# Four groups a turn in TensorE's loop, and the next group's transposes ahead of the last output projection

## The chip, the core and the metric

The kernel runs on one core of a Trainium2 chip. The metric is the device time of one execution in microseconds. A core has five engines that run their own instruction streams and meet only at semaphores: TensorE (PE: matmuls and transposes, which write to the PSUM banks), VectorE (DVE), ScalarE (ACT), GpSimd (POOL) and SyncE (SP), which here issues all the DMAs.

## What is computed

Eight sequences of 1024 tokens with 256 features each go through two "macaron" layers, all in float32:

```
x = x + 0.5 * ffn0(layernorm(x))          # gated silu, hidden size 768
x = x + delta_net(layernorm(x))           # 16 heads, conv, gated recurrence over time, out projection
x = x + 0.5 * ffn0(layernorm(x))
x = x + 0.5 * ffn1(layernorm(x))          # token shift, sigmoid(r) * (relu(k)^2 @ W_v)
x = x + block_attention(layernorm(x))     # 16 heads, rope, causal blocks of 64
x = x + 0.5 * ffn1(layernorm(x))
```

## The kernel before

The 8192 tokens are worked on in 16 groups of 512 tokens, two to a sequence. A group passes through these stages on TensorE, in this order of code:

1. `ffn()`: the normalised rows XN of the group are transposed into PSUM banks 0 and 1 (`transposes()`, eight 128x128 transposes). ScalarE copies bank 0 and VectorE bank 1 into XT (`xt_copy()` on each), and `xt_both()` waits for both copies. Then come the gate and up matmuls of the first feed-forward layer, six times two pairs of 128x512, and the down projection.
2. A second `transposes()` with `xt_both()` for the delta net's input, then the decay inputs and 32 projections with their convolution (`projections`), and the preparation of the chunks' matrices.
3. `recurrence`: eight chunks of 64 tokens, with a chain between TensorE, VectorE and ScalarE. At its end the last chunk's output is normalised by VectorE, transposed by TensorE into bank 2 (`output_t`), copied to VO by ScalarE (`copied()` on TensorE waits for that), and multiplied with WO (`projected(NT - 1)`: 16 matmuls, which the trace shows as 32 records). VectorE adds the result to x, and `added()` on TensorE waits for this addition.

All that comes after the delta net for a group (the second feed-forward layer, the shifted one, the attention and the last one) is called the tail. It is a generator on each engine, cut into 49 pieces, and the pieces of the group before are put into the gaps of the current group's recurrence (`FILL`). All 49 are used up before the last output is transposed, so `for _ in rest` at the end of `recurrence` has nothing left. After the loop the tail of the last group runs by itself.

The next group's x is loaded into R during the recurrence. VectorE takes its statistics before the last output's normalisation and writes XN right behind it (`input_stats`, `input_normal`), ahead of the addition of the last projection.

Loops: TensorE, ScalarE and GpSimd each have a loop of 16 turns with one group a turn. VectorE's has 8 turns of two groups, with two memsets at the head of a turn. SP's has 7 turns of two groups. A loop ends in a branch back to its first instruction. The boundary between two groups is called a seam below. On TensorE it is this order of work:

```
output_t(CHUNKS - 1, 1)
copied()
projected(NT - 1)
added()
pe.wait_ge(s_ready, 2)      # banks 0 and 1 are free again
(branch back)
transposes()                # waits for XN
xt_both()                   # waits for both copies to XT
first gate matmul
```

The loop on TensorE is left after the 16th group; the code behind it starts with two other transposes ("x0f", "x1f") that wait for VectorE's work on the last group.

Of the kernel before, what the change touches and what calls it, by code (L numbers as in the profile page):

```python
# [74 lines left out]
def bass_macaron(nc, x_in, w_gate, w_up, w_down, wq, wk, wv, wab, a_log, dt_bias, wo, conv_w,  # L75
                 w_qk, w_va, w_out, w_r, w_k, w_v, mu, consts, out):
    ctx = ExitStack()
    with ctx:
# [386 lines left out]
        def _(dve):  # L465
# [33 lines left out]
            def input_normal():  # L499
                normal(0, R, XN, xn_ready)  # L500
                normal(1, R, XN, xn_ready)

            def first_ffn(x):
                xt_copy()
                for m in range(HT):
                    s = m % 2
                    dve.wait_ge(th_ready, 1)
                    dve.sem_inc(th_ready, -1)
                    v.scalar_tensor_tensor(FTMP[:, s * G:s * G + G], FTH[:, s * G:s * G + G], 1.0, bank(2 + s),
                                           ALU.add, ALU.mult)  # L510
                    dve.drain()
                    dve.wait_ge(up_ps, 1)
                    dve.sem_inc(up_ps, -1)
                    v.tensor_tensor(out=HH[:, m * G:m * G + G], in0=FTMP[:, s * G:s * G + G], in1=bank(4 + s),
                                    op=ALU.mult).then_inc(h_ready, 1)
                for k in range(2):
                    cols = slice(2 * D * k, 2 * D * k + 2 * D)
                    dve.wait_ge(down_ps, 1)
                    dve.sem_inc(down_ps, -1)
                    if k == 0:  # L520
                        dve.wait_ge(xs_free, 1)
                        dve.sem_inc(xs_free, -1)
                    i = v.scalar_tensor_tensor(x[:, cols], bank(6 + k), 0.25 * W_SCALE ** 3, R[:, cols], ALU.mult, ALU.add)
                    if k == 1:
                        i.then_inc(x_used, 1)
                    dve.drain()
                    stats(k, x)
                for k in range(2):
                    normal(k, x, XN, xn_ready)
# [415 lines left out]
            def recurrence(p):  # L945
                rest = tail(1 - p)

                def fill(n):
                    for _ in range(n):
                        next(rest)  # L950

                fill(FILL_FIRST)
                keys(0)
                for c in range(CHUNKS):
                    right_side(c, 0)
                    right_side(c, 1)
                    fill(FILL[c][0])
                    fill(FILL[c][1])
                    if c >= 5:
                        projected(c - 5, XS[p])  # L960
                    s_update(c, 0)
                    s_update(c, 1)
                    if c + 1 < CHUNKS:
                        keys(c + 1)
                    if c >= 1:
                        mean_square(c - 1)
                    if c == CHUNKS - 1:
                        dve.drain().then_inc(r_free, 1)
                    fill(FILL[c][2])
                    if c >= 1:  # L970
                        normalise(c - 1, 0)
                        normalise(c - 1, 1)
                fill(FILL[CHUNKS][0])
                mean_square(CHUNKS - 1)
                input_stats()
                normalise(CHUNKS - 1, 0)
                normalise(CHUNKS - 1, 1)
                input_normal()
                projected(NT - 1, XS[p])
                dve.drain()  # L980
                for _ in rest:
                    pass
# [11 lines left out]
            dve.drain()  # L994
            input_stats()
            input_normal()
            with dve.Fori(0, B) as b:
                v.memset(S[:, 0:PAIRS * DV], 0.0)
                v.memset(HIST[:, :], 0.0)
                dve.drain()  # L1000
                for p in range(2):
                    first_ffn(XS[p])
                    xt_copy()
                    decay_and_beta()
                    projections(XS[1 - p])
                    recurrence(p)
# [205 lines left out]
        def _(act):  # L1212
# [5 lines left out]
                a.activation(XT[:, 1:G + 1], bank(0), ACT.Copy).then_inc(xt_act, 1)  # L1218

            def ffn():  # L1220
                xt_copy()
                for m in range(HT):
                    s = m % 2
                    act.wait_ge(gate_ps, 1)
                    act.sem_inc(gate_ps, -1)
                    a.activation(FTH[:, s * G:s * G + G], bank(2 + s), ACT.Tanh, scale=0.5 * W_SCALE).then_inc(th_ready, 1)
# [168 lines left out]
            def recurrence():  # L1395
                rest = tail()

                def fill(n):
                    for _ in range(n):
                        next(rest)  # L1400

                def output(c, x):
                    act.wait_ge(ot_ps, 1)
                    act.sem_inc(ot_ps, -1)
                    a.activation(VO[:, :].rearrange("p (n t) -> p n t", n=H)[:, 8 * x:8 * x + 8, c * C:c * C + C],
                                 v3(bank(2), 8), ACT.Copy).then_inc(ot_free, 1)

                def square_out(c, x):
                    act.wait_ge(o_ps, 1)
                    act.sem_inc(o_ps, -1)  # L1410
                    a.activation(SQO[c][:, 512 * x:512 * x + 512], bank(3 + x), ACT.Square).then_inc(sqo_ready, 1)

                fill(FILL_FIRST)
                for y in range(2):
                    inverse_q(y, bank(2 + y))
                for y in range(2):
                    inverse_t(0, y, bank(2 + y))
                for c in range(CHUNKS):
                    if c == 4:
                        inverse_t(1, 1, bank(2))  # L1420
                        act.drain().then_inc(a_done, 1)
                    fill(FILL[c][0])
                    if c >= 2:
                        output(c - 2, 0)
                    if c == 3:
                        inverse_q(0, bank(2))
                    for x in range(2):
                        act.wait_ge(u_ps, 1)
                        act.sem_inc(u_ps, -1)
                        a.activation(US[c % 2][:, 512 * x:512 * x + 512], bank(x), ACT.Copy).then_inc(u_ready, 1)  # L1430
                    if c >= 1:
                        square_out(c - 1, 0)
                    if c >= 2:
                        output(c - 2, 1)
                    if c >= 1:
                        square_out(c - 1, 1)
                    fill(FILL[c][1])
                    if c == 3:
                        inverse_q(1, bank(2))
                    fill(FILL[c][2])  # L1440
                    if c == 3:
                        inverse_t(1, 0, bank(2))
                output(CHUNKS - 2, 0)
                square_out(CHUNKS - 1, 0)
                output(CHUNKS - 2, 1)
                square_out(CHUNKS - 1, 1)
                fill(FILL[CHUNKS][0])
                fill(FILL[CHUNKS][1])
                output(CHUNKS - 1, 0)
                fill(FILL[CHUNKS][2])  # L1450
                output(CHUNKS - 1, 1)
                for _ in rest:
                    pass

            def projections():
                for i in range(CONV_TILES + 5):
# [34 lines left out]

            act.wait_ge(loaded, 16 * N_LOADS)
            a.activation(NEGA[:, :], NEGA[:, :], ACT.Exp).then_inc(nega_ready, 1)
            with act.Fori(0, B * GROUPS) as n:
                ffn()
                xt_copy()
# [14 lines left out]
        def _(pe):  # L1511
# [22 lines left out]
                pe.sem_inc(xt_dve, -1)  # L1534

            def ffn():
                transposes()
                xt_both()
                for m in range(HT):
                    s = m % 2  # L1540
# [375 lines left out]
            def recurrence(rest):  # L1916
# [157 lines left out]
                fill(FILL[CHUNKS][2])  # L2074
                copied()
                output_t(CHUNKS - 1, 1)
                copied()
                projected(NT - 1)
                for _ in rest:
                    pass  # L2080
                added()
                pe.wait_ge(s_ready, 2)
                pe.sem_inc(s_ready, -2)

            pe.wait_ge(loaded, 16 * N_LOADS)
            pe.wait_ge(w_ready, 1)
            pe.sem_inc(w_ready, -1)
            with pe.Fori(0, B * GROUPS) as n:
                ffn()
                transposes()  # L2090
                xt_both()
                pe.wait_ge(qkv_back, 32)
                pe.sem_inc(qkv_back, -32)
                decay_inputs()
                late = tail()
                projections(late)
                pe.wait_ge(b56_free, 2)
                pe.sem_inc(b56_free, -2)
                recurrence(late)
            transposed("x0f", LXN)  # L2100
            transposed("x1f", LXN)
            for _ in tail():
# [72 lines left out]
```

## Time and profile before

| | |
|---|---|
| time, median of 3 runs | 8546.34 us (8544.98 to 8560.92) |
| the profiled execution | 8542.67 us, its span in the profile 8540.9 us |
| busy over the span | PE 81%, PE weight loads 58%, DVE 55%, ACT 31%, POOL 27% |
| mean granted clock of TensorE | 0.901 of full speed |
| DMA | 226 MB, mean 26 GB/s |

In the rows, "PE" is a matmul or transpose, "PEld" the load of its weights, "PEq" and "DVEq" the engine's own sequencer, which is where a wait for a semaphore stands. L1516 is the helper that records every transpose, L1513 the one that records every matmul, so that groups of rows have to be told apart by the tiles they read. A clock of 1.00 is 2.4 GHz, 0.50 is 1.2 GHz.

### The profile page before, as it was taken

Reading aid. Unit: us, or ns where it says so; the run is one execution under the profiler, and the core shown is the slowest. Engines: PE = TensorE matmul, PEld = TensorE weight load, DVE = VectorE, ACT = ScalarE, POOL = GpSimd, SP = SyncE. Lnnn points to the kernel's source line nnn. Section 1 sums busy time; section 2 is a strip of 40 time slices with the busy share of each in tenths; the row PEclk is TensorE's granted clock in tenths of the full one; section 3 lists DMA queues with packets and bytes.
Section 4 is the critical chain, followed back from the end, with each engine's and each line's share of the span. In section 5 each row is a group of like instructions: output and inputs, shape, how many; then the busy total and the mean of one; then the engine's idle time right before and its main releaser. Section 6 shows DMA issues by size and latency. Waiting matters only on the chain. (4 is left out here: it accounts for less than half of the span.)

```text
span 8540.9 us, 157223 instructions
## 1 busy us (share of the span) xinstructions
PE 6906.7 (81%) x57416; PEld 4959.8 (58%) x57416; DVE 4672.3 (55%) x10097; ACT 2617.4 (31%) x5274; POOL 2265.8 (27%) x3555
## 2 busy tenths in 40 slices
PE   7788887888878788887888878788787888878886
PEld 4565646556565565656656466565655656556564
DVE  6446564554645546565465645547455465654643
ACT  3224242332423214232242422324232142322421
POOL 1403223041321413314132230423304133141321
PEclk9898998989989899988989889899898989889898
DMA  1100001001100110000100010011001010011000
GB/s 51 32 25 20 26 28 31 26 20 35 29 20 26 28 36 20 20 31 24 36 20 25 28 31 26 20 35 29 20 26 25 30 28 20 31 24 36 20 25 3
DMA packets 376532, 226.30 MB, mean 26 GB/s; under 512 B 336896, under 2 KB 353920, under 8 KB 367488
## 3 DMA queue, kind: packets, MB, share of 16 engines
q1 hardware_dynamic: 375680, 215.23, 8.7%
q8 instruction: 499, 8.18, 0.4%
q14 instruction: 353, 2.89, 0.1%
HBM read 156.47 MB, written 58.72 MB: 25 GB/s over the span
## 5 line engine op out<-in xcount | busy, mean ns | idle before, releaser
L805 DVE SCALAR_TENSOR_TENSOR PS<-SC,CW,PS 128x512 f32<-128x512 f32 x1536 | 1156.1, 754 | 160.2 <-DVEq L803 79.1
L1516 PE MATMUL PS<-CST,SC 128*128 128x128 f32 x2776 | 466.8, 308 | 511.7 <-PEq L1569 253.6
L1513 PE MATMUL PS<-S,KQ 64*64 64x128 f32 x8192 | 763.2, 308 | 0.0
L1020 POOL TENSOR_TENSOR RSTD<-VAR,NHALF 128x2 f32<-128x2 f32 x202 | 143.0, 708 | 2271.3 <-POOLq L1019 2130.6
L1516 PEld LDWEIGHTS PS<-CST,SC 128*128 128x128 f32 x2776 | 342.9, 155 | 647.1 <-issue 629.0
L1179 POOL TENSOR_TENSOR FR<-MS,NHALF 128x8 f32<-128x8 f32 x128 | 209.9, 1640 | 1504.0 <-POOLq L1178 1298.1
L1513 PEld LDWEIGHTS PS<-S,KQ 64*64 64x64 f32 x8192 | 556.1, 155 | 74.0 <-issue 73.3
L1513 PE MATMUL PS<-XT,WV 128*128 128x512 f32 x1024 | 540.0, 655 | 54.5 <-PEq L1814 54.5
L1513 PE MATMUL PS<-SC 128*64 128x32 f32 (+1 forms) x2720 | 331.7, 332 | 265.2 <-PEq L1638 151.8
L1103 POOL TENSOR_TENSOR WO<-WO 128x30 f32<-128x30 f32 (+14 forms) x960 | 505.6, 527 | 136.4
L1513 PE MATMUL PS<-XT,WQK 128*128 128x512 f32 x1024 | 531.3, 655 | 0.0
L1100 POOL TENSOR_TENSOR WO<-WO 128x30 f32<-128x30 f32 (+14 forms) x960 | 476.6, 497 | 118.4 <-issue 6.9
L1513 PE MATMUL PS<-WO,VO 128*128 128x256 f32 x2048 | 490.9, 401 | 13.9 <-PEq L1974 13.9
L1513 PE MATMUL PS<-WV,SC 64*64 64x128 f32 x8192 | 497.9, 271 | 0.0
L1513 PE MATMUL PS<-XT,WG 128*128 128x256 f32 (+1 forms) x1200 | 437.5, 490 | 65.4 <-PEq L1563 48.4
L1513 PEld LDWEIGHTS PS<-WV,SC 64*64 64x64 f32 x8192 | 446.1, 133 | 34.4 <-issue 31.8
L1513 PEld LDWEIGHTS PS<-WO,VO 128*128 128x128 f32 x2048 | 412.0, 203 | 81.7 <-issue 19.8
L1513 PE MATMUL PS<-SC,CST 128*128 128x512 f32 (+1 forms) x848 | 367.5, 540 | 75.6 <-PEq L1875 48.0
L1513 PE MATMUL PS<-WV,WQK 64*64 64x128 f32 x4096 | 425.2, 287 | 0.0
L1513 PE MATMUL PS<-XT,WU 128*128 128x256 f32 (+1 forms) x1200 | 413.1, 468 | 0.0
L1513 PEld LDWEIGHTS PS<-CST,SC 128*128 128x128 f32 x2048 | 261.0, 198 | 243.3 <-issue 243.2
L1039 POOL TENSOR_TENSOR SC<-SC,CST 128x512 f32<-128x512 f32 x272 | 285.6, 1076 | 377.2 <-POOLq L1070 197.1
(158 smaller groups left out, 12499.2 us busy)
## 6 DMA issues: line engine op xcount, KB each, us to landing
WV<-in_wv SPq DMA_DIRECT2D x16, 2048.0 KB, 7.9
WO<-in_wo SPq DMA_DIRECT2D x16, 2048.0 KB, 7.8
WQK<-in_wq SPq DMA_DIRECT2D x16, 1024.0 KB, 5.2
WQK<-in_wk SPq DMA_DIRECT2D x16, 1024.0 KB, 7.3
cells_in<-SC SPq DMA_DIRECT2D x128, 128.0 KB, 2.6
WO<-cells_in SPq DMA_DIRECT2D x32, 512.0 KB, 3.3
cells_out<-WO SPq DMA_DIRECT2D x32, 512.0 KB, 2.6
cells_nat<-WO SPq DMA_DIRECT2D x32, 512.0 KB, 3.6
```

Source lines behind the costliest of these rows:

```text
L805: op = v.scalar_tensor_tensor(y, pre[:, j:j + G], CW[:, i * TAPS + j:i * TAPS + j + 1], y, ALU.mult, ALU.add)
L1020: q.tensor_tensor(out=RSTD[:, 2 * k:2 * k + 2], in0=VAR[:, 2 * k:2 * k + 2], in1=NHALF[:, 0:2], op=ALU.pow).then_inc(rstd_ready, 1)
L1039: q.tensor_tensor(out=v3(KM[:, n * G:n * G + G], HB), in0=over(KTT[:, at:at + BLK], HB, BLK), in1=each(cst("hmask"), HB, BLK), op=ALU.mult ...
L1100: q.tensor_tensor(out=tmp, in0=each(cells[:, 0:j, j], j, w), in1=over(cells[:, j, j + 1:SUB], j, w), op=ALU.mult)
L1103: q.tensor_tensor(out=cells[:, 0:j, j + 1:SUB], in0=cells[:, 0:j, j + 1:SUB], in1=tmp, op=ALU.add)
L1179: q.tensor_tensor(out=FR[:, :], in0=MS[:, :], in1=NHALF[:, :], op=ALU.pow).then_inc(fr_ready, 1)
L1513: return nc.tensor.matmul(out_, l, r, start=start, stop=stop)
L1516: return nc.tensor.matmul(out_, in_, ident, is_transpose=True, start=True, stop=True)
```

## The change

TensorE's loop body holds four groups, one after the other, and turns four times. The next group's eight transposes of XN move from the head of `ffn()` into the end of `recurrence`, ahead of the wait for ScalarE's copy and of the last output projection; the wait for `s_ready` goes ahead of them. The copies to XT on VectorE and ScalarE move with them: on VectorE between `input_normal()` and the last addition, on ScalarE to the end of its recurrence. The first group's transposes and copies stand ahead of the loops. After the last group one set is done that nobody uses, and one `xt_both()` takes up its semaphores. The loops of the other engines stay as they are.

```diff
@@ VectorE
             def first_ffn(x):
-                xt_copy()
                 for m in range(HT):
@@ VectorE, end of recurrence
                 normalise(CHUNKS - 1, 1)
                 input_normal()
+                xt_copy()
                 projected(NT - 1, XS[p])
                 dve.drain()
@@ VectorE, ahead of the loop
             input_normal()
+            xt_copy()
             with dve.Fori(0, B) as b:
@@ ScalarE
             def ffn():
-                xt_copy()
                 for m in range(HT):
@@ ScalarE, end of recurrence
                 output(CHUNKS - 1, 1)
                 for _ in rest:
                     pass
+                xt_copy()
@@ ScalarE, ahead of the loop
+            xt_copy()
             with act.Fori(0, B * GROUPS) as n:
                 ffn()
@@ TensorE
             def ffn():
-                transposes()
                 xt_both()
@@ TensorE, end of recurrence
                 output_t(CHUNKS - 1, 1)
+                for _ in rest:
+                    pass
+                pe.wait_ge(s_ready, 2)
+                pe.sem_inc(s_ready, -2)
+                transposes()
                 copied()
                 projected(NT - 1)
-                for _ in rest:
-                    pass
                 added()
-                pe.wait_ge(s_ready, 2)
-                pe.sem_inc(s_ready, -2)
@@ TensorE, the loop
-            with pe.Fori(0, B * GROUPS) as n:
-                ffn()
-                transposes()
-                xt_both()
-                ...
-                recurrence(late)
+            transposes()
+            with pe.Fori(0, B * GROUPS // 4) as n:
+                for _ in range(4):
+                    ffn()
+                    transposes()
+                    xt_both()
+                    ...
+                    recurrence(late)
+            xt_both()
             transposed("x0f", LXN)
```

## Rows read from the trace of the kernel before

**Rows 1.** The page: busy time, share of the span and instructions of each engine

```profile
PE 6906.7 (81%) x57416; PEld 4959.8 (58%) x57416; DVE 4672.3 (55%) x10097; ACT 2617.4 (31%) x5274; POOL 2265.8 (27%) x3555
```

**Rows 2.** Waits of TensorE: us in total, times, longest us

```profile
PE PS L1516 <- PEq L1524: 157.3, 48, 39.0
```

**Rows 3.** Windows, seam to seam: length, busy times, clock, DMA share, GB/s

```profile
1078.85:1597.70 518.85, 422.66 (x3554) 303.89 (x3555) 285.82 (x619) 161.60 (x326) 139.79 (x220) 0.90 0.09 27
...
3673.05:4195.24 522.19, 426.28 (x3555) 305.80 (x3555) 286.26 (x619) 161.51 (x326) 139.68 (x220) 0.90 0.09 26
```

**Rows 4.** Timeline of TensorE, first seam, then second and last: start, us, [idle before]

```profile
544.20 1.09 PE L1516 MATMUL PS<-CST,WV 128*128 128x128 f32 x4 [1.02 <-PEq L1967]
546.15 9.38 PE L1513 MATMUL PS<-WO,VO 128*128 128x256 f32 x32 [0.87 <-PEq L1974]
560.06 1.14 PE L1516 MATMUL PS<-CST,SC 128*128 128x128 f32 x8 [4.53 <-PEq L1524]
562.18 3.75 PE L1513 MATMUL PS<-XT,WG 128*128 128x512 f32 x4 [0.99 <-PEq L1534]
...
568.46 1.88 PE L1513 MATMUL PS<-XT,WG 128*128 128x512 f32 x4
570.17 1.88 PE L1513 MATMUL PS<-XT,WU 128*128 128x512 f32 x4
...
1080.94 3.75 PE L1513 MATMUL PS<-XT,WG 128*128 128x512 f32 x4 [0.98 <-PEq L1534]
...
7830.44 1.13 PE L1516 MATMUL PS<-CST,SC 128*128 128x128 f32 x8 [4.50 <-PEq L1524]
```

**Rows 5.** Timeline of VectorE, first seam

```profile
538.73 0.75 DVE L472 BATCH_NORM_STATS2 BST<-WV 128x6 f32<-128x256 f32 x2 [0.20 <-DVEq L495]
...
542.46 1.38 DVE L485 TENSOR_SCALAR SC<-WV,MVR,RSTD 128x256 f32<-128x256 f32 x4
555.68 0.42 DVE L943 TENSOR_TENSOR XB<-XB,PS 128x256 f32<-128x256 f32 x1 [11.85 <-DVEq L941]
561.35 0.69 DVE L491 COPY XT<-PS 128x512 f32<-128x512 f32 x1 [5.24 <-DVEq L490]
```

**Rows 6.** Timeline of ScalarE, first seam

```profile
545.41 0.60 ACT L1405 ACTIVATE VO<-PS 128x512 f32<-128x512 f32 x1 [1.51 <-ACTq L1404]
561.14 0.60 ACT L1218 ACTIVATE XT<-PS 128x512 f32<-128x512 f32 x1 [15.14 <-ACTq L1217]
```

**Rows 7.** Windows at the first seam; the last three columns: PEclk, DMA share, GB/s

```profile
541.00:546.10 5.10, 2.17 (x8) 1.43 (x8) 2.76 (x8) 1.19 (x2) 0.70 (x2) 0.50 0.01 3
546.10:555.50 9.40, 9.35 (x32) 7.59 (x32) 0.00 (x0) 0.00 (x0) 0.00 (x0) 0.76 0.59 225
555.50:560.00 4.50, 0.03 (x1) 0.00 (x0) 0.42 (x1) 0.00 (x0) 0.00 (x0) 1.00 0.01 4
...
562.20:568.40 6.20, 6.20 (x8) 2.67 (x9) 0.69 (x1) 0.60 (x1) 0.00 (x0) 0.55 0.00 0
```

**Rows 8.** Timeline of VectorE, second seam, where its own loop turns

```profile
1074.51 0.42 DVE L943 TENSOR_TENSOR XB<-XB,PS 128x256 f32<-128x256 f32 x1 [11.85 <-DVEq L941]
1078.39 0.91 DVE L998 MEMSET S<- 128x1024 f32 x1 [3.46 <-issue]
...
1085.56 0.69 DVE L509 SCALAR_TENSOR_TENSOR SC<-SC,PS 128x512 f32<-128x512 f32 x1 [4.77 <-DVEq L508]
```

**Rows 9.** Timeline of VectorE where its loop has ended, behind the last addition

```profile
8345.59 0.75 DVE L472 BATCH_NORM_STATS2 BST<-XB 128x6 f32<-128x256 f32 x2 [0.25 <-issue]
```

**Rows 10.** The page: the DMA queue of instructions: packets, MB, share of 16 engines

```profile
q8 instruction: 499, 8.18, 0.4%
```

**Rows 11.** Timeline of TensorE: an output projection inside the recurrence

```profile
8304.70 7.07 PE L1513 MATMUL PS<-WO,VO 128*128 128x256 f32 x32
```

**Rows 12.** SyncE: the load of the next x, its issue and its landing

```profile
527.49 0.40 SPq L367 DMA_DIRECT2D WV<-in_x  x1
...
DMA to landing us min/median/max: 3.6/4.2/4.6
```

More of the change, by code:

```diff
@@ L2087, in _ @@
             pe.sem_inc(w_ready, -1)
-            with pe.Fori(0, B * GROUPS) as n:
-                ffn()
-                transposes()
-                xt_both()
[L2092 to L2098, printed above, removed]
-                recurrence(late)
+            transposes()
[4 more added lines that the diff above has]
+                    xt_both()
+                    pe.wait_ge(qkv_back, 32)
+                    pe.sem_inc(qkv_back, -32)
+                    decay_inputs()
+                    late = tail()
+                    projections(late)
+                    pe.wait_ge(b56_free, 2)
+                    pe.sem_inc(b56_free, -2)
+                    recurrence(late)
+            xt_both()
             transposed("x0f", LXN)
```

## Prediction

> **What bounds the kernel now.** I read the page's busy times first, for the engine with the least room; then TensorE's waits by line; then its timeline over one seam between two groups, with VectorE's and ScalarE's beside it; then the clock in windows; last the places that price a loop turn. The chain of waits that ended last is of no use here: it stops 0.9 us before the end. TensorE is busy 81% of the span, VectorE 55% [rows 1], and TensorE's order of work spans the groups. Every turn of its loop looks alike: of the 14 stretches from one seam's transposes to the next, 12 last 518.7 to 519.0 us and two 522.2 [rows 3]. So I price one seam and multiply.
>
> The wait before a seam's transposes (L1524) costs 157.3 us in 48 pieces [rows 2]. 39.0 of it is the start; the 15 seams take 4.5 us each, some 68 us, and the rest is the second set of transposes of each group, which stays. At a seam TensorE does this [rows 4]: the last output transposes at 544.20, the last output projection from 546.15 to 555.53, nothing for 4.53 us, eight transposes at 560.06, 0.99 us of waiting for the copies of XT, first gate matmul at 562.18. All 15 look so; the last stands beside the first in [rows 4].
>
> What holds the transposes back? Not their input: VectorE wrote the last of XN at 542.46 + 1.38 = 543.84. VectorE's addition, for which `added()` waits, ends at 555.68 + 0.42 = 556.10 [rows 5]. Between it and 560.06 lie 3.96 us in which nothing is owed to TensorE. What stands there is the loop's branch. VectorE has the same thing in its own loop, of two groups a turn: after the addition at 1074.51 its next instruction, a memset that waits for nothing, starts 3.46 us late [rows 8]. Where the loop ends and it runs straight on, the next instruction follows the addition after 0.25 us [rows 9]. So a branch back costs about 3.5 us and going straight on about nothing. In the stretch of TensorE's idle time the DMA engines moved 4 GB/s x 4.5 us = 18 KB [rows 7], near the 8.18 MB / 499 = 16.4 KB of one packet of the instruction queue [rows 10].
>
> The Trainium skill, Runtime: NRT & Kernel Launch, section Instruction fetch mechanics, says that a taken branch whose target isn't held on chip waits for a fetch; the trace agrees. The Trainium skill, Advanced Engine Details and Errata, section Control Flow Timing, gives about 0.11 us for a compare-and-branch; by that figure, an estimate, 12 branches would be worth 1.3 us, and the 3.46 and 3.96 us above speak against it.
>
> **The loop of four groups.** Of the 15 seams, 12 become straight code and 3 keep the branch. Removed on a straight seam is the 3.96 us; what follows the addition is then limited by the semaphore. After VectorE's copy of XT (561.35 + 0.69 = 562.04 [rows 5]) the gate matmul started at 562.18 [rows 4], 0.14 us later; I take that.
>
> **The transposes moved ahead.** Eight transposes, ScalarE's copy and VectorE's copy leave the place after the branch and go in front of the last projection. Nothing of it is a DMA. SP's and GpSimd's queues are not touched; both have the same instructions in the same order. The first gate matmul no longer waits for copies: 562.18 - 560.06 = 2.12 us gone from each of the 15 seams. What they cost in the new place: they can start when output transposes are issued. These began at 544.20 and their row lasts 1.09 us, to 545.29; the projection began at 546.15, behind ScalarE's copy, which ended at 545.41 + 0.60 = 546.01 [rows 4, 6]. So 0.86 us of the new work is covered by a gap. Eight transposes took 1.14 us behind the branch, and four took 1.09 where the granted clock was 0.50 [rows 4, 7]. Bounds of the shift of the projection: nothing (all in the gap) and 2 x 1.09 - 0.86 = 1.3 us. I take 0.5, as the four-transpose row holds one latency that isn't paid twice. If the cover went, it would be 1.4 to 2.2 us instead. The bank copies and the XT copies then lie under 9.4 us of projection. VectorE gets its copy between the normalisation and the addition, where it waited 11.85 us [rows 5]; behind that new wait stands only the addition, which needs the projection anyway. ScalarE has 15 us idle there too [rows 6].
>
> `added()` now stands directly ahead of the gates: projection's end to addition's start 0.15 us, addition 0.42, semaphore 0.14, together 0.71 us exposed. So on a straight seam the first gate comes at 555.53 + 0.5 + 0.71 = 556.74 in place of 562.18: **5.44 us**. On a branching seam the 3.96 us stay, and it comes at 560.06 + 0.5 = 560.56: **1.62 us**. I count no loss for VectorE's own branch: at every second seam its memset would start 1078.39 - 1074.51 - 0.42 = 3.46 us after the addition and end about 1 us later, 4.5 us after it; its first feed-forward work came 1085.56 - 1080.94 = 4.6 us after the first gate with a slow clock, so about 3 us with a fast one [rows 4, 8]. That is up to 1.5 us late, while TensorE needs its result only after eight more records (6.9 us after the first gate).
>
> **The clock.** The granted clock in the idle 4.5 us was still 1.00, fell after it, and was 0.55 over the first gates [rows 7]: 2.4 GHz gave way to 1.2. The first eight gate and up records took 568.46 - 562.18 = 6.28 us; the next four took 1.71, so eight at full clock are 3.42 [rows 4]. Loss **2.86 us** at each seam. On a straight seam the idle time shrinks to 0.71 us. TensorE had idle pieces of 0.87 and 0.99 at the seam, but these don't decide anything alone; that the clock fell behind 4.53 us and not before is what the rows show. I count the 2.86 us as won on the 12, as lost still on the 3. The clock also was 0.50 up to the projection, which took 9.38 us against 7.07 for 32 such records at full clock [rows 4, 7, 11]: 2.31 us more that the fuller gap before it might win; I count nothing. The Trainium skill, TensorE: Matmul & The Clock Gate, section Part 4: PE-mode transpose, says that transposes don't count towards raising the clock as matmuls do; no run here shows it yet, and by it this extra would be zero, the rest of the sum unchanged.
>
> **The sum.** 12 x (5.44 + 2.86) = 99.6; 3 x 1.62 = 4.9; after the last group the eight transposes are new work with nobody to use them, - 0.5. Together 104 us. The profiled execution took 8542.7 us (span 8540.9): 8438.7. The median of the runs is 3.7 above it: **8442 us**, 1.2% faster.
>
> **Why the size is uncertain.** The turns came in two lengths 3.4 us apart with nothing between [rows 3]. A turn's length moves in steps, and 8.3 us could show as two steps (6.8) or three (10.2). Twelve of these are 82 or 122 us; the three branching seams give 0 or one step, up to 10. So the forecast's own range is a gain of 82 to 132: 8414 to 8464. The rest of a turn also has stretches of slow clock that may now lie elsewhere, with either sign.
>
> **Rivals.**
> Gates stay slow. If 0.71 us of idle time beside the earlier gaps is enough to bring 1.2 GHz at the gates, 2.86 x 12 goes: 70 us, 8476. For it: the clock was low until 546. Against: it was 0.76 on average over the projection, so high in its second half, and 1.00 after. Chance 0.14.
> The projection speeds up as well. With transposes in its gap the clock would rise earlier on all 15 seams: 15 x 2.31 = 35 more, 8408. Against: transposes are little work. Chance 0.09.
> The straight seam stalls as before, because the 3.96 us is no branch but something in the order of work, or because straight code at that place waits for its instructions too. Then all 15 seams gain 1.62: 24 us, 8522. Against: [rows 8, 9]. This is also the rival that the unrolling does nothing. Chance 0.05. The Trainium skill's Control Flow Timing, named above, would have it so.
> Slower. The transposes now stand ahead of the projection and wait for XN. If the next group's x came late, the projection, its addition and the whole next group would wait. It decides only when XN is ready (104 + 17) / 15 = 8 us later than TensorE's 545.3, at 553; it is ready at 543.84, margin 1.4 us, and the load that feeds it is issued at 527.49 and lands after 3.6 to 4.6 us, so at least 6.6 us before VectorE first reads it at 538.7 [rows 5, 12]. At 12 us late, 15 x 12 - 104 = 76 us slower, 8622. Chance 0.02.
>
> **How the numbers follow.** Forecast 0.67, the four rivals 0.30, anything else 0.03. The range takes in the first two rivals and the bounds of the shift: 8405 to 8480. No change, for this kernel, is what lies within 0.2% (17 us). Faster 0.94 (all but the late x, half of the unnamed rest, and a part of the stalling seam), same 0.04, slower 0.02.
>
> **What would show it.** In the timeline of a straight seam: eight transposes between the last output transposes and the projection, about 1 us idle or less before the first gate, gates at 1.71 us per four from the start. At the seams after groups 4, 8 and 12: still some 4.5 us idle and slow gates. TensorE's wait at L1524's successor falls by some 60 us. The prediction is wrong if a 4 us gap stands at straight seams, if the clock is low at their gates, or if turns are not about 510.5 us long.

## The result, and the profile of the changed kernel

The changed kernel takes 8402.92 us, median of 4 runs (8400.02 to 8413.74), against 8548.22 us for the kernel before (4 runs): ratio 0.9832, 95% interval 0.9821 to 0.9844. That is 145 us less. The forecast was 104 us less, 8442 us, with a range down to 8405; the time lies just under the range. The profiled execution took 8403.19 us, 139.5 us less than the profiled one of before.

The page of the changed kernel, the instruction queue, and two waits of TensorE (L1526 is now the wait for XN in `transposes()`, L1536 that of `xt_both()`). They answer to [rows 1, 2, 10]:

```profile
PE 6851.6 (82%) x57424; PEld 4944.2 (59%) x57424; DVE 4672.8 (56%) x10098; ACT 2616.4 (31%) x5275; POOL 2266.4 (27%) x3555
...
q8 instruction: 475, 7.78, 0.4%
```

```profile
PE PS L1518 <- PEq L1526: 89.8, 33, 38.9
...
PE PS L1515 <- PEq L1536: 27.3, 16, 4.8
```

The wait for XN fell by 157.3 - 89.8 = 67.5 us; the 33 pieces left are the start and the second transposes of the groups. At the three branching seams the stall has moved: it stands ahead of the gates now, in the second of the two lines. 24 packets of instructions fewer were fetched, two for each of the 12 branches that are gone.

The first seam, a straight one (no branch between its two groups), and the fourth, where the loop turns, in TensorE's timeline; both answer to [rows 4]:

```profile
542.80 1.09 PE L1518 MATMUL PS<-CST,WV 128*128 128x128 f32 x4 [1.02 <-PEq L1968]
543.68 1.91 PE L1518 MATMUL PS<-CST,SC 128*128 128x128 f32 x8
545.38 7.30 PE L1515 MATMUL PS<-WO,VO 128*128 128x256 f32 x32
553.71 1.96 PE L1515 MATMUL PS<-XT,WG 128*128 128x512 f32 x4 [1.03 <-PEq L1536]
555.50 1.88 PE L1515 MATMUL PS<-XT,WU 128*128 128x512 f32 x4
557.22 1.88 PE L1515 MATMUL PS<-XT,WG 128*128 128x512 f32 x4
...
2072.82 1.92 PE L1518 MATMUL PS<-CST,SC 128*128 128x128 f32 x8
2074.53 7.31 PE L1515 MATMUL PS<-WO,VO 128*128 128x256 f32 x32
2086.46 3.75 PE L1515 MATMUL PS<-XT,WG 128*128 128x512 f32 x4 [4.62 <-PEq L1536]
2090.00 2.91 PE L1515 MATMUL PS<-XT,WU 128*128 128x512 f32 x4
2092.75 1.45 PE L1515 MATMUL PS<-XT,WG 128*128 128x512 f32 x3
```

The eight transposes stand ahead of the projection. At the straight seam 1.03 us lie between projection and gates and the gates run at full speed; at the fourth there are 4.62 us, and the first eight gate and up records take 6.3 us. What the forecast didn't count is the projection: 7.3 us at every seam, in place of 9.4. The clock in windows at the first seam (the last three columns: PEclk, DMA share, GB/s; they answer to [rows 7]):

```profile
542.00:545.30 3.30, 2.50 (x12) 2.53 (x13) 0.43 (x2) 1.10 (x2) 0.00 (x0) 0.50 0.01 2
545.30:552.70 7.40, 7.38 (x34) 6.14 (x32) 0.69 (x1) 0.60 (x1) 0.00 (x0) 0.96 0.73 280
...
553.70:560.00 6.30, 6.29 (x15) 2.92 (x16) 1.40 (x3) 1.19 (x2) 0.00 (x0) 1.00 0.00 0
```

Over the projection the mean granted clock is 0.96, where it was 0.76. The turns, from seam to seam (length, PE busy, PEclk, DMA share, GB/s), answer to [rows 3]; the third one begins at a seam that still branches:

```profile
542.80:1054.74 511.94, 422.02 (x3554) 0.91 0.09 27
1054.74:1563.49 508.75, 418.94 (x3555) 0.91 0.09 27
2071.94:2587.38 515.44, 422.25 (x3554) 0.91 0.09 27
```

Of the 15 turns eleven are 508.4 to 508.8 us long, one 511.9 and three 515.4 to 515.5. Before, measured in the same way, 13 were 518.7 to 518.9 and two 522.2. All these lengths lie some 3.4 us apart.

VectorE's own branch, at the second seam, comes as forecast; it answers to [rows 8]:

```profile
1064.80 0.42 DVE L942 TENSOR_TENSOR XB<-XB,PS 128x256 f32<-128x256 f32 x1 [6.43 <-DVEq L940]
1068.47 0.91 DVE L999 MEMSET S<- 128x1024 f32 x1 [3.25 <-issue]
...
1069.67 0.69 DVE L508 SCALAR_TENSOR_TENSOR SC<-SC,PS 128x512 f32<-128x512 f32 x1 [0.19 <-DVEq L507]
```

It makes the first feed-forward work late: VectorE begins it 4.0 us after the first gate matmul, at the first seam 2.8 us after it. VectorE catches up before TensorE needs the result: the gates of the second seam ran at the same pace as those of the first.

### The profile page after: what moved, and what is told of

Same layout as the page of the kernel before. It is cut to its first block and busy times, and to the rows that moved or that the text cites. A ratio compares the mean times of both kernels' runs of the same rounds, so it can differ in the third digit from the quotient of the medians.

```text
span 8401.4 us, 157225 instructions
## 1 busy us (share of the span) xinstructions
PE 6851.6 (82%) x57424; PEld 4944.2 (59%) x57424; DVE 4672.8 (56%) x10098; ACT 2616.4 (31%) x5275; POOL 2266.4 (27%) x3555
## 5 line engine op out<-in xcount | busy, mean ns | idle before, releaser
L1518 PEld LDWEIGHTS PS<-CST,SC 128*128 128x128 f32 x2784 | 355.8, 159 | 569.8 <-issue 551.0
L1104 POOL TENSOR_TENSOR WO<-WO 128x30 f32<-128x30 f32 (+14 forms) x960 | 508.8, 530 | 136.5
L1515 PE MATMUL PS<-XT,WG 128*128 128x256 f32 (+1 forms) x1200 | 413.2, 468 | 76.6 <-PEq L1564 48.4
L1515 PE MATMUL PS<-WO,VO 128*128 128x256 f32 x2048 | 457.7, 382 | 0.0
L1515 PEld LDWEIGHTS PS<-WO,VO 128*128 128x128 f32 x2048 | 390.9, 192 | 52.8
L1515 PEld LDWEIGHTS PS<-CST,SC 128*128 128x128 f32 x2048 | 279.2, 208 | 228.7 <-issue 228.3
## 6 DMA issues: line engine op xcount, KB each, us to landing
WO<-cells_in SPq DMA_DIRECT2D x32, 512.0 KB, 3.4
cells_out<-WO SPq DMA_DIRECT2D x32, 512.0 KB, 2.6
cells_nat<-WO SPq DMA_DIRECT2D x32, 512.0 KB, 3.6
```

Source lines behind the costliest of these rows:

```text
L1104: q.tensor_tensor(out=cells[:, 0:j, j + 1:SUB], in0=cells[:, 0:j, j + 1:SUB], in1=tmp, op=ALU.add)
L1515: return nc.tensor.matmul(out_, l, r, start=start, stop=stop)
L1518: return nc.tensor.matmul(out_, in_, ident, is_transpose=True, start=True, stop=True)
```

## The experiments

Two theories were open. The one of the forecast prices a seam: the branch of 3.96 us, the waits for the copies, the clock of the gates, with the projection untouched. Its rival says that work in the gap ahead of the projection (0.87 us of idle time before the change) brings the full clock to it earlier. A third question came with the turn lengths: whether what is won at a seam is won at all.

### Each half alone

`unroll_only` has the loop of four on the kernel before, with the transposes behind the projection. `move_only` has the moved transposes in a loop of one group.

```diff
 unroll_only, against the kernel before
-            with pe.Fori(0, B * GROUPS) as n:
-                ffn()
+            with pe.Fori(0, B * GROUPS // 4) as n:
+                for _ in range(4):
+                    ffn()
...
 move_only, against the changed kernel
-            with pe.Fori(0, B * GROUPS // 4) as n:
-                for _ in range(4):
-                    ffn()
+            with pe.Fori(0, B * GROUPS) as n:
+                ffn()
```

> The kernel before with four groups a turn in TensorE's loop, the transposes left behind the last projection. The 12 straight seams should lose the 3.96 us of the branch, and their gates should run at full clock (2.86 us each): 12 x 6.8 = 82 us, 8466 us. The last projection should stay at 9.4 us, if it is the transposes in front of it that made it 7.3 us long in the changed kernel. If it was only the other rhythm of the turns that did it, it is shorter here too on most seams, and the time is nearer 8440. If straight seams stall as before, no change.

> The changed kernel with one group a turn: every seam has the branch and the transposes in front of the projection. If the moved transposes alone shorten the projection, all 15 turns are as long as the three branching ones of the changed kernel, 515.4 us in place of 518.9: 15 x 3.4 = 51 us, 8497 us. If the projection stays at 9.4 us, only the waits at the gates go: 15 x 1.3 = 20 us, 8528 us.

`unroll_only` took 8477.1 us, ratio 0.9915 (0.9900 to 0.9931), 73 us less than before. `move_only` took 8513.4 us, ratio 0.9953 (0.9938 to 0.9968), 37 us less. Both fall short of what was expected (82 and 51 us). Together they give 110, while both in one give 145. Two seams of `unroll_only`, the first and the second:

```profile
546.09 9.38 PE L1513 MATMUL PS<-WO,VO 128*128 128x256 f32 x32 [0.87 <-PEq L1974]
556.49 1.07 PE L1516 MATMUL PS<-CST,SC 128*128 128x128 f32 x8 [1.02 <-PEq L1524]
558.54 1.96 PE L1513 MATMUL PS<-XT,WG 128*128 128x512 f32 x4 [0.99 <-PEq L1534]
...
1061.50 9.38 PE L1513 MATMUL PS<-WO,VO 128*128 128x256 f32 x32 [0.87 <-PEq L1974]
1071.90 1.07 PE L1516 MATMUL PS<-CST,SC 128*128 128x128 f32 x8 [1.02 <-PEq L1524]
1076.76 3.40 PE L1513 MATMUL PS<-XT,WG 128*128 128x512 f32 x4 [3.79 <-PEq L1534]
```

Behind the projection 1.02 us are left of 4.53: the branch was the stall, and 3.5 us is its net cost. The projection stays at 9.38 us, although the turns here have other lengths (511.8 to 518.9). So the rhythm of the turns did not shorten it in the changed kernel. The second seam shows a wait that the forecast had not named for this half: 3.79 us for the copies, and slow gates behind it. There VectorE turns its own loop, and the copy of XT stands behind that branch and the two memsets. The copy of the first seam, then the second seam:

```profile
557.70 0.69 DVE L491 COPY XT<-PS 128x512 f32<-128x512 f32 x1 [1.67 <-DVEq L490]
...
1071.03 0.42 DVE L943 TENSOR_TENSOR XB<-XB,PS 128x256 f32<-128x256 f32 x1 [11.85 <-DVEq L941]
1074.72 0.91 DVE L998 MEMSET S<- 128x1024 f32 x1 [3.27 <-issue]
...
1075.92 0.69 DVE L491 COPY XT<-PS 128x512 f32<-128x512 f32 x1 [0.19 <-DVEq L490]
```

The move takes the copy in front of VectorE's branch, so the two halves need each other at the four straight seams where VectorE branches. In `move_only` the projection takes 7.3 us at all 16 places, and the way from the output transposes through the first eight gate and up records is some 3.3 us shorter at each seam. Yet ten turns of 15 are as long as before, 518.7 to 518.9; only five are a step shorter. Its first projection, and one turn of each length:

```profile
544.82 7.31 PE L1515 MATMUL PS<-WO,VO 128*128 128x256 f32 x32
...
2615.44:3134.17 518.73, 424.91 (x3555) 0.90 0.09 27
3134.17:3649.67 515.50, 422.63 (x3554) 0.91 0.09 27
```

### No branch, and a branch in idle time

`unroll16` has all 16 groups in straight code. `rotated` keeps one group a turn, but puts the branch ahead of the last output transposes, where TensorE waits 5.4 us for the normalisation in any case.

```diff
 unroll16
-            with pe.Fori(0, B * GROUPS // 4) as n:
-                for _ in range(4):
+            for _ in range(B * GROUPS):
...
 rotated: last_output() is copied(), output_t x2, transposes(), projected(NT - 1), added();
 group() is all the rest of a group
+            group()
+            with pe.Fori(0, B * GROUPS - 1) as n:
+                last_output()
+                group()
+            last_output()
```

> The changed kernel with no loop on TensorE. The three seams that still branched become straight: 515.4 - 508.6 = 6.9 us each, 21 us in all, 8382 us. If straight code of this length had to wait for its instructions somewhere, the gain would be smaller or negative and idle pieces of issue would show on TensorE.

> One group a turn, but the branch stands ahead of the last output transposes, where TensorE waits 5.4 us for VectorE anyway. If the branch is a delay of 3.5 to 4 us that starts when the sequencer reaches it, it is hidden there on all 15 seams and the time is that of the kernel without a loop, 8382 us. If the fetch can't start before the matmuls ahead of it have run, or costs more there, every seam shows a part of it, up to 15 x 6.9 - 21 = 82 us more, 8485.

`unroll16` took 8383.5 us, ratio 0.9805 (0.9791 to 0.9818), and `rotated` 8385.3 us, ratio 0.9807 (0.9794 to 0.9820): both as expected, 19 and 18 us below the changed kernel. In the fourth seam of `rotated` nothing of the branch is to be seen; the wait before the output transposes is the same 5.37 us as everywhere:

```profile
2072.51 1.09 PE L1518 MATMUL PS<-CST,WV 128*128 128x128 f32 x4 [5.37 <-PEq L1968]
...
2077.21 7.32 PE L1515 MATMUL PS<-WO,VO 128*128 128x256 f32 x32
2085.55 1.96 PE L1515 MATMUL PS<-XT,WG 128*128 128x512 f32 x4 [1.02 <-PEq L1536]
...
q8 instruction: 497, 8.14, 0.4%
```

The last line is the instruction queue of `rotated`: 497 packets, against 499 before and 471 in `unroll16`. The branches still fetch, only in time that was idle anyway. So this branch, which cost 3.5 us at the seam, costs nothing inside a 5.4 us wait of its engine, and the loop need not be unrolled to be rid of it.

### What shortens the projection

Three kernels, each against the kernel before. `dummy_tr8` and `dummy_mm4` add work to TensorE whose results nobody reads; `delay_only` adds idle time by doing ScalarE's last copy twice.

```diff
 dummy_tr8 (dummy_mm4: four times mm(..., cst("ones"), cst("later")))
                 output_t(CHUNKS - 1, 1)
+                pe.wait_ge(s_ready, 2)
+                pe.sem_inc(s_ready, -2)
+                for i in range(8):
+                    tr(bank(i % 2)[:, 0:P], cst("later"))
                 copied()
                 projected(NT - 1)
...
                 added()
-                pe.wait_ge(s_ready, 2)
-                pe.sem_inc(s_ready, -2)
```

> The kernel before, with eight transposes of a constant into banks 0 and 1 put in front of the last output projection, whose results nobody reads; the real transposes stay behind the branch. If it is work in the gap that brings the full clock earlier, and transposes count as such work, the projection takes 7.3 us instead of 9.4 at every seam, although each seam does more than before: 0.6 later, 2.1 shorter, 15 x 1.5 = 22 us faster at most, less where turns move only in steps of 3.4 us. If transposes don't count, 9.4 us stay and the time is up to 10 us longer.

> The same with four plain matmuls of 128 columns (eight records) in place of the eight transposes. If any work counts, the projection takes 7.3 us as with the transposes. If only plain matmuls count, 7.3 us here and 9.4 with the transposes.

> The kernel before, with ScalarE's last copy of the output done twice, so that the projection starts some 0.7 us later while TensorE stays idle. If it is only the moment at which the projection starts that decides how much of it runs at the slow clock, it takes 7.3 us here too. If it is the work in front of it, it stays at 9.4 us, and the time rises by 15 x 0.7 = 10 us, or by steps of 3.4 us in some turns.

| kernel | median us | ratio (95%) | projection, first seam |
|---|---|---|---|
| dummy_tr8 | 8529.1 | 0.9974 (0.9964 to 0.9984) | 7.31 us |
| dummy_mm4 | 8528.8 | 0.9974 (0.9964 to 0.9984) | 7.27 us |
| delay_only | 8549.5 | 1.0001 (0.9991 to 1.0010) | 9.02 us |

The first seam of `dummy_tr8`, of `dummy_mm4` and of `delay_only`, one fence each; the x8 rows are the unread work:

```profile
547.07 1.92 PE L1516 MATMUL PS<-CST 128*128 128x128 f32 x8
548.78 7.31 PE L1513 MATMUL PS<-WO,VO 128*128 128x256 f32 x32
```

```profile
545.72 1.92 PE L1513 MATMUL PS<-CST 128*128 128x128 f32 x8
547.43 7.27 PE L1513 MATMUL PS<-WO,VO 128*128 128x256 f32 x32
```

```profile
546.05 9.02 PE L1519 MATMUL PS<-WO,VO 128*128 128x256 f32 x32 [1.59 <-PEq L1980]
```

It is the work. A delay of 0.7 us with TensorE idle takes only 0.36 us off the projection, eight records of unread work take 2.1, and they start it no later than that delay does (2.59 us behind the second output transposes, against 2.67). A kernel that does more became 22 us faster. Transposes do it as well as matmuls do. About half of what the projection gains, 16 x 2.1 = 33 us, is lost again behind it: in `dummy_tr8` the way from the output transposes through the first eight gate and up records is 2.1 us shorter than before at six seams, and only 0.1 to 0.3 us at the other nine.

### Less waiting, more time

The last three kernels go at waits near the seam. `early_stats`, on `rotated`, moves VectorE's statistics of the next x ahead of the last mean square. `filled_gap`, on `unroll16`, puts 24 transposes that nobody reads at the start of the 5.4 us wait; the wait for `s_ready` moves ahead of them. `unroll_pe_dve`, on `unroll_only`, unrolls VectorE's loop as well.

```diff
 early_stats
-                mean_square(CHUNKS - 1)
                 input_stats()
+                mean_square(CHUNKS - 1)
...
 filled_gap, ahead of the last output transposes
+                pe.wait_ge(s_ready, 2)
+                pe.sem_inc(s_ready, -2)
+                for i in range(24):
+                    tr(bank(i % 2)[:, 0:P], cst("later"))
...
 unroll_pe_dve
-            with dve.Fori(0, B) as b:
+            for _ in range(B):
```

> The rotated loop, and VectorE's statistics of the next x put ahead of the last mean square, where it waits some 4.6 us for nothing else, instead of between the mean square and the normalisation. The normalisation then waits for GpSimd's power alone and comes 0.9 us earlier at each seam. If turns were free to shorten: 16 x 0.9 = 14 us less than the rotated kernel, 8371 us. If a turn only moves in steps of 3.4 us, either nothing on most turns (8385) or a step on some or all of them (down to 8334).

> The kernel without a TensorE loop, with 24 transposes of a constant at the start of the 5.4 us in which TensorE waits for the last normalisation; nobody reads them. If work in idle time keeps the clock up, the output transposes and the projection behind them run at 2.4 GHz from the start (7.0 us for the projection in place of 7.3, some 1 us less for the transposes). Each seam is then up to 1.5 us shorter, 24 us in all if turns could shorten freely (8360); with turns that move in steps of 3.4 us, anything from 8384 to 8335. If the gap is too long for 24 of them, nothing changes at the seam.

> The kernel of unroll_only with VectorE's loop unrolled too, so that no branch of VectorE stands at a seam. In unroll_only the seams where VectorE branches left 5.8 to 7.4 us between projection and first gate, the others 3.1 us. If that difference is VectorE's branch and memsets, which the copy of XT stands behind, all straight seams now show 3.1 us and gates at full clock; six seams (the eighth, fourth and twelfth keep TensorE's branch, so 2, 6, 10 and 14 in particular) gain 3 to 4 us each, 12 to 20 us in all: 8460 us. If it has another cause, 8477 stays.

None of the three won time, and the first two came out slower than anything that was expected of them. `early_stats`: the wait ahead of the output transposes fell from 5.37 to 4.61 us, but the projection took 7.6 to 7.7 us in place of 7.3, and the kernel took 8415.2 us, ratio 0.9842 (0.9828 to 0.9855), some 30 us more than `rotated`. `filled_gap`: the first output transposes took 0.63 us in place of 1.09, and the kernel took 8426.9 us, ratio 0.9861 (0.9844 to 0.9877), 43 us more than `unroll16`. Its projection was slower, not faster (7.5 to 7.7 us): the 24 transposes ran early and 2.59 us of idle time were left behind them. `unroll_pe_dve` did win what it was made for: all straight seams but one (3.4) had the 3.1 us that were expected between projection and first gate. Yet the kernel took 8485.2 us, ratio 0.9931 (0.9914 to 0.9948), where 8460 was expected; it is not faster than `unroll_only` with 0.9915 (0.9900 to 0.9931), and the two intervals overlap. The 24 transposes and the wait behind them in `filled_gap`, and the wait and the projection in `early_stats`:

```profile
534.46 2.84 PE L1518 MATMUL PS<-CST 128*128 128x128 f32 x24
539.90 0.63 PE L1518 MATMUL PS<-CST,WV 128*128 128x128 f32 x4 [2.59 <-PEq L1968]
```

```profile
540.31 1.08 PE L1518 MATMUL PS<-CST,WV 128*128 128x128 f32 x4 [4.61 <-PEq L1968]
...
545.09 7.64 PE L1515 MATMUL PS<-WO,VO 128*128 128x256 f32 x32
```

Where the time went can be read in windows. The same three stretches of a turn, with the same 361, 881 and 2315 records, first in `rotated`, then in `early_stats`:

```profile
1563.96:1673.66 109.70, 99.63 (x361) 0.92 0.10 39
1673.66:1813.86 140.20, 115.13 (x881) 0.91 0.13 29
1813.86:2072.51 258.65, 204.31 (x2315) 0.92 0.07 21
```

```profile
1052.28:1161.52 109.24, 99.27 (x361) 0.93 0.10 39
1161.52:1305.58 144.06, 118.72 (x881) 0.88 0.13 29
1305.58:1564.30 258.72, 205.27 (x2315) 0.91 0.07 21
```

The wait that was cut stands at the end of the third stretch, and in this pair that stretch is no shorter for it. The second, the late projections and the preparation of the chunks, 110 to 250 us behind the seam, with no line of code changed in it, is 3.9 us longer at a mean clock of 0.88 in place of 0.91. The turn is 3.5 us longer in all. Over all turns the picture is the same, if less sharp: in the ten long turns of `early_stats` the second stretch took 144 to 145 us at 0.87 to 0.88, in the 15 turns of `rotated` 140 to 143 at 0.90 to 0.91. Ten of the 15 turns of `early_stats` are 511.9 to 512.0 us long and five 508.6; in `rotated` four are 511.9 to 512.0 and eleven 508.5 to 508.7. In `filled_gap` 14 of 15 are 511.9 to 512.1, in `unroll16` three of 15.

## Why the prediction was wrong

**The stall at the seam is the branch.** Right. 3.96 us per branch were priced; `unroll_only` shows 1.02 us in place of 4.53 with nothing moved, the fourth seam of the changed kernel still shows 4.62, and `unroll16` removes that one. Net of the semaphore wait that takes its place, the branch cost 3.5 us. The Trainium skill, Runtime: NRT & Kernel Launch, section Instruction fetch mechanics, says that a taken branch to a target that isn't held on chip waits for a fetch; the trace agrees, with two packets fewer for each branch removed. (The 18 KB that the prediction read beside one packet were those in the idle stretch; the count makes it two for a branch.) The 0.11 us of the Trainium skill, Advanced Engine Details and Errata, section Control Flow Timing, do not hold for these branches, back over a whole group.

**The waits at the gates.** Right, within 0.4 us. From the second set of output transposes to the projection: 545.38 - 542.80 = 2.58 us against 1.95 before, a shift of 0.63 (0.5 taken). Projection's end to gate: 1.03 us (0.71 taken); the addition ended at 552.83 + 0.42 = 553.25 (the line below), and from there to the gate it was 0.46 us and not 0.14.

```profile
552.83 0.42 DVE L942 TENSOR_TENSOR XB<-XB,PS 128x256 f32<-128x256 f32 x1 [6.40 <-DVEq L940]
```

**The clock of the gates.** Right: 553.71 to 557.22 is 3.51 us for eight records, 6.28 before, at the straight seams; slow still at the three others.

**The projection's clock.** This is the step that failed: "2.31 us more that the fuller gap before it might win; I count nothing". The runs show 7.3 us at every seam in place of 9.38: it won some 2.08 us at all 15 seams and at the last place too, 16 x 2.08 = 33 us. The case was the second rival, given 0.09, with 8408 us against the 8403 measured. The choice rested on "transposes are little work"; `dummy_tr8` shows that eight of them, with 9.38 us turned into 7.31, are enough. The Trainium skill, TensorE: Matmul & The Clock Gate, section Part 4: PE-mode transpose, says that transposes don't count as matmuls do, and the prediction noted that by it the extra would be zero. `dummy_tr8` and `dummy_mm4`, 7.31 and 7.27 us, show no difference between them; here the measurement decides against the rule.

**The sum by seams.** From the first set of output transposes to the ninth gate or up record it was 26.4 us before and is 16.5 on a straight seam: 9.8 (8.3 forecast). On a branching seam it is 22.9: 3.4 (1.62 forecast). 12 x 9.8 + 3 x 3.4, and 1.8 behind the last group, are 130 us, against 104. 33 of these 26 + 9 us that the forecast lacks are the projection. The smaller terms of a seam came out 7 us below the forecast in all, and the other 9 us of the 139.5 lie elsewhere in the turns: the two turns of 522.2 us, a step above their neighbours, have gone (6.7 us), one straight turn, of 511.9, stayed a step above its own (3.4 us the other way), and the rest is spread over the turns. The 7 and the 9 nearly cancel, so that the rival's 8408 lies so near the 8403 measured is in part luck.

**Steps.** "8.3 us could show as two steps or three" held: eleven of the twelve straight turns got 10.3 us shorter, three steps, one 6.9, and the branching ones 3.4. The prediction's own sign of being wrong came true as well: eleven of the twelve straight turns are 508.6 us long and not about 510.5. But I used the steps only to widen a range. What `move_only`, `early_stats` and `filled_gap` show is stronger: a turn can take none of what its seam gives. 3.3 us won locally gave nothing on ten turns of 15.

**Rivals.** The stalling straight seam, the slow gates and the late x did not come: TensorE's transposes at 543.68 followed the output transposes with no wait.

**What stays open.** The clock in a stretch far from the edit is shown to differ; why the turns fall into those lengths is not. The lengths 3.4 us apart held in the other kernels, but not in `unroll_pe_dve`, which has turns of 513.4, 514.4, 517.4 and 519.9 us, so they are a habit of these programs and no law. Whether filler work at another place, in the 110 to 250 us behind a seam, would win there wasn't tried.

## What to carry to other kernels

Look for a group of idle time with no releaser but "issue", or a wait whose semaphores are all long in, at the head of a loop: here it was 3.2 to 4 us from the end of the last work to the next instruction, for each branch back on TensorE and on VectorE. On TensorE it cost nothing once the loop was rotated so that the branch fell where the engine waits anyway, which did as well as unrolling 16 times. When work is moved into idle time ahead of matmuls, count the matmuls behind it as faster too, if the clock was at its low level there; unread work in that place shows how much before anything is moved. The place matters: 24 transposes at the start of a 5.4 us wait made the kernel 43 us slower. And where the granted clock changes many times in a loop, a local gain of a few microseconds doesn't even fix the sign: `early_stats` won 0.76 us of waiting at each seam and lost 30 us. Price the seam, then let a run tell what the turn makes of it.

## What was not expected of the hardware

Unread work made the kernel faster: eight extra transposes or four extra matmuls at each seam, 22 us less in all (0.9974). Removing 0.76 us of waiting at each seam made it 30 us slower: 140 to 143 us of unchanged work far behind the seam took 144 to 145 in the long turns, at a mean clock of 0.87 to 0.88 in place of 0.90 to 0.91. And in `unroll_only` VectorE's copy began 4.0 us after the transposes at the seam where VectorE branches, against 1.2 us at the first, and TensorE waited for it; the same branch cost TensorE nothing once the copy had been moved ahead of it.
